# Key products of the block inverses computed per batch, chunk and head inside the projection stage

## The reference, cut to what matters

```python
q = rope((x @ Wq)...);  k = rope(l2norm((x @ Wk)...));  v = (x @ Wv)...
beta = 2 * sigmoid(x @ Wb)
# in chunks, for each batch and head:
A  = tril(einsum('bhik,bhjk->bhij', K, K) * beta[..., None, :], -1)
Vn = solve_triangular(eye + A, V - K @ S, lower=True)
S  = S + (K * beta).T @ Vn
# then causal softmax attention with q, k * beta and the new v, then @ Wo
```

## Time and profile before

| | |
|---|---|
| median of 3 runs | 991.86 us (989.54 to 999.53) |
| profiled execution | 987.09 us, its span 985.4 us |
| TensorE busy | 834.9 us (85%) |
| VectorE busy | 602.9 us (61%) |
| ScalarE busy | 458.6 us (47%) |
| GpSimd busy | 285.5 us (29%) |
| granted TensorE clock, mean of the span | 0.887 of full |

### The profile page before, as it was taken

The page is one execution under the profiler, slowest core; times in us unless marked ns, Lnnn a source line. Parts: engine busy times, 40 slices in busy tenths (PEclk is TensorE's granted clock), DMA queues, the critical chain, the costliest instruction groups (busy, mean ns, idle before and its releaser), DMA issues. The chain is left out here.

```text
span 985.4 us, 23672 instructions
## 1 busy us (share of the span) xinstructions
PE 834.9 (85%) x9023; PEld 590.4 (60%) x9023; DVE 602.9 (61%) x2051; ACT 458.6 (47%) x1082; POOL 285.5 (29%) x533
## 2 busy tenths in 40 slices
PE   6894843688889999989998889959899999997784
PEld 3563733677766666668894455534466666586362
DVE  1786589277778999735434535440389999384264
ACT  2564521100017777743335775563257777564054
POOL 0772230275633333310003100000033333511535
PEclk9996556799979999998988998969789999996798
DMA  6044562333410730030001000000000000290561
GB/s 131 1 107 85 150 187 87 98 94 95 98 25 2 211 93 1 3 97 2 1 1 29 0 0 1 1 1 0 1 1 2 2 3 2 59 282 21 209 228 48
DMA packets 54904, 60.55 MB, mean 61 GB/s; under 512 B 9129, under 2 KB 40327, under 8 KB 54536
## 3 DMA queue, kind: packets, MB, share of 16 engines
q1 hardware_dynamic: 45768, 47.46, 17.9%
q10 hardware_dynamic: 6640, 5.27, 1.9%
q0 software_dynamic: 2384, 6.31, 1.7%
HBM read 29.75 MB, written 25.99 MB: 57 GB/s over the span
## 5 line engine op out<-in xcount | busy, mean ns | idle before, releaser
L905 DVE CUSTOM_DVE_ANT_0 l_masked_scores<-psum,mask_q_rows 128x384 bf16<-128x384 f32 (+3 forms) x512 | 220.6, 487 | 31.0 <-PE psum L845 27.4
L921 ACT ACTIVATE kT_or_probs<-psum 128x512 f32<-128x512 f32 (+1 forms) x192 | 87.2, 529 | 115.4 <-PE psum L831 114.2
L934 POOL TENSOR_SCALAR_AFFINE_SELECT l_probs<-l_probs 128x256 f32<-128x256 f32 x128 | 50.5, 407 | 227.5 <-ACT l_probs L921 227.3
L921 ACT ACTIVATE l_probs<-psum 128x512 f32<-128x512 f32 (+1 forms) x192 | 87.1, 529 | 33.1 <-PE psum L831 31.9
L845 PE MATMUL psum<-l_k_heads,l_q_heads 32*128 32x512 f32 (+3 forms) x512 | 93.8, 485 | 2.4 <-PEq L46 1.5
L845 PE MATMUL psum<-kb_heads,q_heads 32*128 32x384 f32 (+3 forms) x512 | 93.2, 481 | 1.9 <-DVE l_neg_max_rows L905 1.0
L831 PE MATMUL psum<-l_q_and_max,kb_heads 32*128 32x512 f32 (+3 forms) x512 | 87.9, 460 | 0.7 <-DVE l_q_and_max L911 0.7
L831 PE MATMUL psum<-l_q_and_max,l_k_heads 32*128 32x512 f32 (+3 forms) x512 | 87.8, 459 | 0.7 <-DVE l_q_and_max L911 0.7
L934 POOL TENSOR_SCALAR_AFFINE_SELECT kT_or_probs<-kT_or_probs 128x256 f32<-128x256 f32 x128 | 50.5, 406 | 95.1 <-ACT kT_or_probs L921 95.0
L845 PEld LDWEIGHTS psum<-l_k_heads,l_q_heads 32*128 32x128 f32 x512 | 57.6, 196 | 10.2 <-DVE l_neg_max_rows L905 3.8
L678 POOL TENSOR_TENSOR v_new_and_ones<-v_and_k_rows_or_heads 32x128 f32<-32x128 f32 x128 | 55.1, 447 | 27.0 <-DVE v_and_k_rows_or_heads L656 20.7
(11 more groups left out here) (359 smaller groups left out, 1821.1 us busy)
## 6 DMA issues: line engine op xcount, KB each, us to landing
sorted_scratch<-l1p_zeros SPq DMA_DIRECT2D x23, 257.0 KB, 6.3
gram_scratch<-rows_32k SPq DMA_DIRECT2D x4, 1024.0 KB, 4.9
rows_32k<-v_new_and_ones SPq DMA_DIRECT2D x64, 64.0 KB, 2.5
x_rows<-in_L_attn_x_dram SPq DMA_DIRECT2D x16, 128.0 KB, 6.7
heads_scratch<-rows_32k SPq DMA_DIRECT2D x2, 1024.0 KB, 5.4
heads_scratch<-q_kb_T SPq DMA_DIRECT2D x2, 1024.0 KB, 5.9
inverse_scratch<-block_inv SPq DMA_DIRECT2D x2, 1024.0 KB, 4.0
q_heads<-heads_scratch SPq DMA_DIRECT2D x8, 256.0 KB, 3.5
```

What stands on the lines that cost most here:

```text
L905: last = self.nc.vector.tensor_tensor_reduce(out=self.junk[:, n % 4, o:o + w], in0=self.g.ps[:, self.row_bank(G, u, i), o:o + w], in1=self ...
L921: self.nc.scalar.activation(self.PT[:, G % 2, 2 * (u % 2) + i, o:o + w], self.g.ps[:, self.e_bank(G, u, i), 0:w], ACT.Exp, scale=SCALE).th ...
L934: last = self.nc.gpsimd.affine_select(out=d, in_=d, pattern=[[0, 2], [1, P]], compare_op=ALU.is_ge, fill=0.0, base=0, channel_multiplier=-1)
```

## The change

The key products move from the start of the block stage into the last part of the projection stage. There they are made by group of four chunks, `gram(q)`: one call for each chunk c, x, batch b and head row j, on a 32 x 32 tile of the array (rows of head j, columns of batch b) with 16 rows of keys, 32 columns of weights and 32 moving columns. That is 256 calls a group and 1024 in all, where before there were 256 calls of 16 x 128 x 128. Head row j writes bank j, batch b its own 32 partitions, so each group fills four whole banks with wanted squares only. A group is copied out by `gram_rows` in four pieces of 128 x 512: groups 0 to 2 all on ScalarE, group 3 two on ScalarE and two on VectorE. `store_gram` stores each group (1024 KB); SyncE issues groups 0 to 2 and the beta loads before the last heads, ScalarE issues group 3 ahead of its two stores of heads. `block_A` is laid out with all 16 heads in one row of 256 elements and is loaded in 16 transfers (8 on SyncE, 8 on ScalarE; half of them 12 chunks = 192 KB, half 4 chunks = 64 KB), and VectorE waits for all of them before the first scaling. The waits of `heads_stored` move from inside the key-product loops to the head of ScalarE's program.

```diff
@@ phase_qkv
+        AT = [g.kt_or_probs[:, HG * NT * P:], w_xT[:, 0:4 * 2 * D], g.rows32k[:, 0:4 * 2 * D], g.rows32k[:, 4 * 2 * D:8 * 2 * D]]
+        def gram_rows(copy, q, j):
+            return copy(AT[q].rearrange("p (f k j m) -> p j k f m", f=2, k=G4 * HG, j=4)[:, j, :, :, :], ps[:, j, :].rearrange("p (k f m) -> p k f m", f=2, m=CH))
+        def store_gram(eng, q):
+            dst = bass.AP(tensor=g.gram_d.tensor, offset=g.gram_d.offset + q * G4 * D, ap=[[2 * NT * D, P], [NT * D, 2], [1, G4 * D]])
+            eng.dma_start(dst, AT[q].rearrange("p (f n) -> p f n", f=2)).then_inc(g.gram_st[q], 16)
@@ SyncE, in the loop over groups q
                 if q == LAST:
                     sp.wait_ge(beta_ok, 2 * NG)
                     sp.dma_start(g.beta_d, ...).then_inc(g.beta_st, 16)
+                    for n in range(LAST):
+                        sp.wait_ge(at_ok[0], 4 * (n + 1))
+                        store_gram(sp, n)
+                    sp.wait_ge(g.beta_st, 16)
+                    ...                      # the 8 loads of beta, from the block stage
                 sp.wait_ge(qt_sb, G4 * (q + 1))
                 store_heads(sp, q, 0, 0, P)
@@ ScalarE, at the end of each turn c of its loop, and after the loop
+                if NT < c < NT + 4:
+                    act.wait_ge(gram_ps, c - NT)
+                    if c == NT + 3:
+                        act.wait_ge(kn_ok, LAST)
+                    for n in range(4):
+                        gram_rows(nc.scalar.copy, c - NT - 1, n).then_inc(at_ok[0], 1)
+            act.wait_ge(gram_ps, NG)
+            for n in range(2):
+                gram_rows(nc.scalar.copy, LAST, n).then_inc(at_ok[0], 1)
+            act.wait_ge(at_ok[0], 4 * LAST + 2)
+            act.wait_ge(at_ok[1], 2)
+            store_gram(act, LAST)
             act.wait_ge(kk_sb, 2 * G4 * NG)
             for j in (2, 3):
                 store_heads(act, LAST, 1, SLOT * j + HD, HD)
@@ VectorE, after its loop
+            dve.wait_ge(gram_ps, NG)
+            for n in range(2, 4):
+                gram_rows(nc.vector.tensor_copy, LAST, n).then_inc(at_ok[1], 1)
@@ TensorE
+            def gram(q):
+                pe.wait_ge(kk_sb, 2 * G4 * (q + 1))
+                if q == 0:
+                    pe.wait_ge(xT_sb, NT)
+                    pe.wait_ge(qk_sb, NT)
+                else:
+                    pe.wait_ge(at_ok[0], 4 * q)
+                for c in range(G4):
+                    for x in range(HG):
+                        o = (HG * c + x) * R
+                        for b in range(B):
+                            for j in range(4):
+                                kt = g.KT[SLOT * j:SLOT * j + HD, x, G4 * q + c, R * b:R * b + R]
+                                last = nc.tensor.matmul(ps[R * b:R * b + R, j, o:o + R], kt, kt, start=True, stop=True)
+                last.then_inc(gram_ps, 1)
             for c in range(NT + KLAG):
...
+                if c == NT + 3:
+                    k_heads(c - KLAG)
+                    gram(c - NT - 1)
                 if QLAG <= c < NT + QLAG:
                     q_heads(c - QLAG)
-                if KLAG <= c:
+                if KLAG <= c and c != NT + 3:
                     k_heads(c - KLAG)
+                if c in (NT + 1, NT + 2):
+                    gram(c - NT - 1)
+            gram(LAST)
@@ delta_blocks: the L466 loop, both diagonal() loops, the stores of L575 and the beta loads are removed
-        def load_blocks(eng, x, hf):
-            for i in range(2):
-                eng.wait_ge(gram_st[2 * x + i], 16)
-            for b in range(B):
...
+        def load_blocks(eng, b0):
+            for c0, c1 in ((0, NT - G4), (NT - G4, NT)):
+                for q in range(c0 // G4, c1 // G4):
+                    eng.wait_ge(g.gram_st[q], 16)
+                for b in (b0, b0 + 1):
+                    for hf in range(2):
...
+                        eng.dma_start(L[p0 + 2 * c0:p0 + 2 * c1 - 1:2, :, :, :].rearrange("p j h i -> p j (h i)"), src).then_inc(l_ok, 16)
@@ VectorE of delta_blocks
+            dve.wait_ge(g.bl_ok, 16 * 2 * B)
+            dve.wait_ge(l_ok, 16 * 4 * B)
             for x in range(2):
-                dve.wait_ge(l_ok[x], 16 * 2 * B)
@@ ScalarE of delta_blocks
+            for i in range(2):
+                heads_stored(act, g, i)
+            load_blocks(act, 2)
@@ SyncE of delta_blocks
             for i in range(2):
                 heads_stored(sp, g, i)
+            load_blocks(sp, 0)
```

More of the change, by code:

```diff
@@ L118, in phase_qkv @@
         qT_ps, kT_ps, kk_sb, qt_sb = sem("qT_psum"), sem("kT_and_kbT_psum"), sem("kT_and_kbT_sbuf"), sem("qT_sbuf")
+        gram_ps, at_ok = sem("gram_psum"), [sem(f"gram_blocks{i}") for i in range(2)]
         ps = g.ps
@@ L416, in delta_blocks @@
         block = ctx.enter_context(nc.Block())
[L418 to L421, removed]
         def uw_rows(copy, u):
@@ L457, in _ @@
             for u in range(2 * NP):
[L458 to L470, removed]
                 n, x = u // 2, u // NP
@@ L485, in _ @@
         def _(dve):
[L486 to L492, removed]
+            dve.wait_ge(g.bl_ok, 16 * 2 * B)
+            dve.wait_ge(l_ok, 16 * 4 * B)
             for x in range(2):
-                dve.wait_ge(l_ok[x], 16 * 2 * B)
                 for j in range(0, CH, 4):
-                    lj = L[:, x, j:j + 4, :, j + 1:]
+                    lj = L[:, j:j + 4, H2 * x:H2 * x + H2, j + 1:]
                     nc.vector.tensor_tensor(lj, lj, bcast(bl[:, j:j + 4, H2 * x:H2 * x + H2], [[H, 4], [1, H2], [0, CH - 1 - j]]), ALU.mult).then_inc(la_ok, 1)
@@ L518, in _ @@
         def _(act):
-            for u in range(2 * NP):
-                act.wait_ge(gram_ps, u + 1)
-                if u == NP:
-                    heads_stored(act, g, 0)
-                for b in range(2, B):
-                    diagonal(nc.scalar.copy, u, b).then_inc(at_ok[1], 1)
-            load_blocks(act, 1, 1)
+            for i in range(2):
+                heads_stored(act, g, i)
+            load_blocks(act, 2)
             load_inverse(act, 0, 1)
@@ L549, in _ @@
             nc.gpsimd.memset(VC[:, :, :, :], 1.0).then_inc(start_ok, 1)
+            for q in (2, 3):
+                pool.wait_ge(g.gram_st[q], 16)
             for x in range(2):
-                for i in range(2):
-                    pool.wait_ge(gram_st[2 * x + i], 16)
                 nc.gpsimd.memset(g.rows32k[:, 4 * P * H2 * x:4 * P * H2 * (x + 1)], 0.0).then_inc(td_zero, 1)
@@ L557, in _ @@
             pool.wait_ge(t_step, 2 * STEPS)
-            nc.gpsimd.memset(L[:, :, :, :, :], 0.0).then_inc(td_zero, 1)
+            nc.gpsimd.memset(L[:, :, :, :], 0.0).then_inc(td_zero, 1)
         @block.sync
@@ L2379, in program @@
             g.vec_rows = sb2("vector_rows", [NVEC, P])
+            g.gram_st, g.bl_ok = [ctx.enter_context(nc.semaphore(f"gram_stored{q}")) for q in range(NG)], ctx.enter_context(nc.semaphore("block_beta_loaded"))
             with ExitStack() as c3:
```

44 lines of the change are left out of this document (15 added, 29 removed).

## The result

The changed kernel takes 1038.8 us (median of 4 runs, 1033.48 to 1045.1) against 993.3 for the kernel before on the same chips. The ratio is 1.0454, with a 95% interval of 1.0372 to 1.0536. It is slower, as forecast, but by 45 us where I had said 13, and 1038.8 lies above the upper end of the range, 1034. The profiled execution has a span of 1038.3 us, 52.9 more than before; the medians differ by 45.5, so some 7 us of the difference between the two traces is spread from execution to execution.

A forecast was written before the change was run, and what follows sets the result against it. TensorE was taken to bound the key-product stage (29.04 of 30.6 us) ahead of the first scaling. -15.9 + 28.9 gave +13 us: 991.9 + 12.9 = 1005 us, own range 998 to 1012, range asked for 984 to 1034.

The forecast's parts named there:

- the 6.98 us of idle time: TensorE's idle stretch before the q_heads at 81.17, ahead of gram(0); forecast as not used.
- the distances between the groups: Time on the path between the four gram groups, forecast as 2.4 + 4.6 + 10.3 us.
- the 12.4 named for the half clock: Upper value for gram(2) to gram(3) if all runs at half clock; 10.3 us was taken, 9.7 at full clock.
- tail and loads: Path from gram(3) to the first scaling: 9.7 us for copies, stores and landing, then 8.5 us for loading block_A.
- -15.9 + 4 G: Forecast change in us at the first scaling, from 134.53 to 118.6 + 4 G; no change at G = 4.0 us.
- G: TensorE's time for one group of key products (256 calls, 512 records); taken as 7.2 us, forecast range 5.5 to 9.
- the burst's 14.1 ns: Time per record in a 16-record burst of 64-column products in the kernel before, taken as the price of gram's records.
- Rival 2: Only instruction fetching binds gram: four packets of 1.1 us, 4.5 us a group; sum +2, 994 us; chance 0.22.
- Rival 1: Issue or decode bounds gram's stream: 27.3 ns a record, 14.0 us a group; sum +40, 1032 us; chance 0.27.
- There is room: Claim that block_A's 2 MB load in 8.5 us at 247 GB/s, since 197 GB/s took a share of 0.62.
- Rival 3: Gram's tiles run side by side, 1.8 us a group; sum -8.7, or -10.2 (982 us) with 7 us loads; chance 0.13.
- F: Theory of the follow-up runs, not the forecast: gram is bound by instructions, 256 arriving every 3.45 us or later.

The follow-up runs named there:

- e4_loads: Changed kernel with block_A loaded in 8 transfers of 16 chunks instead of 8 of 12 and 8 of 4: 1030.2 us, ratio 1.043.
- e7_quiet: Changed kernel with SyncE's store of the third group's heads held until ScalarE has copied groups 0 to 2: 1035.2 us, ratio 1.0451.
- e10_quarter: Kernel before with 4 of its 16 key-product units moved into projection-stage idle time, first copy earlier, the quarter's store later: 982.3 us against 987.5.
- e3_half: Changed kernel with half of the key products (every second x), each with 64 moving columns: 1008.3 us, ratio 1.0173.

## Why the prediction was wrong

**What held.** The moment to argue about was the first scaling, and nothing behind it changed. TensorE's order made the groups additive: the 6.98 us of idle time went unused, and the distances between the groups came to 18.3 us against 17.3 (the third took 12.0 us, near the 12.4 named for the half clock, and 0.50 is what was granted). What was hidden before lay bare afterwards: tail and loads, 24.6 us where the forecast had 18.2. No engine or queue that I had priced at nothing came onto the path. The sign followed from -15.9 + 4 G with any G above 4.

**What failed: the price of G.** The forecast took "the burst's 14.1 ns" for a stream of 512 records and got 7.2 us. The four groups took 12.4 to 16.1, 56.3 instead of 28.9, which is 27 of the 37 us missed. The pace inside a burst was even better than taken, 10.2 ns. What I left out of the forecast's case is that a burst ends: after 256 instructions the next ones are not there. Rival 2 had this mechanism and the count of packets right (four a group) and its price wrong, 4.5 us a group (four packets of 1.1 us make 4.4). It took the 1.1 us in which a packet is moved for the time from packet to packet. That time is 3.45 us at the least, of which the move is 0.9 to 1.1 us; the rest passes without any transfer, as the DMA view of 90 to 97.3 us shows, which has two packets and nothing else. Rival 1 had the value, 14.0 us a group, and was right that the burst's pace does not last. But its price is luck. L479's 27.3 ns, over 128 records, come to 3.49 us, close to the time of a packet, and yet L479 has no gaps between packets: ahead of its two entries in the earlier trace rows TensorE's timeline of the kernel before has

```profile
179.52 6.49 PE L479 MATMUL psum<-rows_32k,v_and_k_rows_or_heads 128*32 128x128 f32 x128 [6.68 <-DMA rows_32k<-inverse_scratch]
```

and from there 256 records follow one another to 189.5 us without a gap, where `gram` would have one after every 128. No run shows what bounds L479, nor a link between the two figures.

The spacing of starts in `gram` is 10.2 ns within a burst; 3.45 us / 128 = 27 ns holds only on average over packets.

**The second term: the loads.** "There is room" was read from a share of 0.62 with transfers to 16 partitions each. The change cut them into transfers to 12 and 4 partitions, a detail that I named in the description and did not price. It cost 5 us by e4_loads, through few engines at work, through more time for issuing, or both; the other 2 us of the miss are there with 16 partitions too, where the share reached 1.02.

**The range.** It took rival 1's value as its edge and had 7 us of loads and 2 us of start beyond it. Rival 3 (the tiles side by side in 1.8 us) has no support at all: even without gaps a group would need 512 x 10.2 = 5.2 us.

**What stays open.** No run put idle instructions into the stream at a price low enough to lengthen the packets' count by itself; F rests on the bursts of exactly 128 records, on the packets 2.2 to 2.7 us ahead of every burst that follows a gap, on their counts (76, 84 and 88) and on e7_quiet. Why the next packet does not come earlier, and what passes between its end and the next burst, the traces do not show.

## What to carry to other kernels

Count TensorE's instructions as well as its columns. Here a product and its weight load in float32 are four instructions, 256 instructions arrived every 3.45 us at best, and beside large transfers they came later (gaps of 2.4 to 4.1 us instead of about 2). By an estimate from these numbers (4 x 3.45 us / 256) that is 54 ns a call, and the calls of `gram`, whose two records take 20 ns within a burst, waited for their instructions. Price a long stream from a long stream and never from a burst, and where a page of the profile has bytes of instructions, look for the time from packet to packet, not for that of the packet. To use the idle time of an in-order engine, put work ahead of the wait that ends it: behind that wait `gram(0)` left the 6.98 us whole, and four units of the old products, put ahead of such waits in e10_quarter, were worth 7 us on the path in its trace and about 5 us in the median.

## What the runs showed of the hardware

- Instructions of TensorE arrived in packets of 256 (2,048 fewer instructions and 8 fewer packets in e3_half; 1.38 MB in the changed kernel's 84 packets, 16 KB each). In the stream of `gram` a burst of 256 followed the last in 3.45 us or more. With DMA traffic at a share of 0.62 to 0.82 beside them the gaps grew from about 2 us to between 2.4 and 4.1, `gram(2)` from 12.0 us (share 0.02, e7_quiet) to 16.1 (0.62, changed kernel) and `gram(3)` from 13.1 (0.29, changed kernel) to 17.4 (0.82, e7_quiet). The packet's own transfer stayed at about 0.9 us of DMA engine time in the one looked at; it started later, 3.3 us after the start of a burst instead of 1.1 to 1.4.
- Products on 32 x 32 tiles with 32 columns started 10.2 ns apart within a burst at a granted clock of 0.50; with 64 columns a burst of 128 took 1.97 us instead of 1.54, and with 32 columns at a granted clock of 1.00 it took 1.27.
- A separate increment of a semaphore ahead of each product on TensorE made a call cost 153 ns.
- 2 MB loaded in 16 transfers to 12 and 4 partitions took 15.7 us, in 8 transfers to 16 partitions 10.5.
